# Two transformer layers on one core: in layer 0, exponential before the query's high part, row sum before its low part

## The reference, cut to what matters

```python
q = (query @ Wq + bq).reshape(B, Sq, H, D)
k = (key @ Wk + bk).reshape(B, Sk, H, D)
v = (value @ Wv + bv).reshape(B, Sk, H, D)
scores = jnp.einsum('bqhd,bkhd->bhqk', q, k) * scale
mask = (key_mask == 0)[:, None, None, :]
scores = jnp.where(mask, jnp.float32(-1000000000.0), scores)
probs = jax.nn.softmax(scores, axis=-1)
ctx = jnp.einsum('bhqk,bkhd->bqhd', probs, v).reshape(B, Sq, H * D)
return ctx @ Wo + bo
```

## Time and profile before

| | |
|---|---|
| median of 3 runs | 2923.28 us (2917.49 to 2926.4) |
| the profiled execution's own time | 2921.61 us |
| its span, first to last instruction | 2919.8 us |
| TensorE busy | 2646.1 us (91%) |
| VectorE busy | 2023.6 us (69%) |
| ScalarE busy | 1517.6 us (52%) |
| GpSimd busy | 1522.0 us (52%) |
| TensorE clock granted, mean | 0.953 |

### The profile page before, as it was taken

How to read it: one execution, slowest core, us unless ns; L and a number is a source line. 1 busy time by engine, 2 the same in 40 slices (tenths; PEclk the granted TensorE clock), 3 DMA queues, 4 the chain that set the end, 5 groups by cost and what they waited for, 6 DMA issues and landing times. The chain is left out here.

```text
span 2919.8 us, 41005 instructions
## 1 busy us (share of the span) xinstructions
PE 2646.1 (91%) x14566; PEld 2188.7 (75%) x14566; DVE 2023.6 (69%) x4005; ACT 1517.6 (52%) x2897; POOL 1522.0 (52%) x1149
## 2 busy tenths in 40 slices
PE   6699999986778699999999999999999998799698
PEld 5577777763436588888888888888888887677476
DVE  3677777742546377777777777777777777577666
ACT  2234334331213277777777777777777777111175
POOL 2355544320000166666666666666666666465555
PEclk9899999998878899999999999999999999899899
DMA  5212222133348633334333343233433314668475
GB/s 188 56 54 56 56 57 57 41 96 128 139 145 312 228 74 80 106 83 115 81 77 109 80 118 81 75 111 76 122 80 77 109 51 136 210 238 288 157 275 187
DMA packets 212526, 351.15 MB, mean 120 GB/s; under 512 B 75839, under 2 KB 82370, under 8 KB 204631
## 3 DMA queue, kind: packets, MB, share of 16 engines
q1 hardware_dynamic: 193539, 284.89, 32.8%
q0 software_dynamic: 11680, 45.02, 4.2%
q10 hardware_dynamic: 7104, 18.61, 1.6%
HBM read 172.47 MB, written 156.64 MB: 113 GB/s over the span
## 5 line engine op out<-in xcount | busy, mean ns | idle before, releaser
L1880 POOL TENSOR_SCALAR pa_Pr<-pa_Pr,pa_rs 128x590 f32<-128x590 f32 x512 | 902.4, 1769 | 485.1 <-DVE pa_rs L2109 484.9
L2113 DVE TENSOR_REDUCE pa_least<-pa_S 128x1 f32<-128x590 f32 x512 | 390.7, 763 | 230.0 <-PE pa_S L1944 227.9
L2034 ACT ACTIVATE pa_Pr<-pa_S,pa_least 128x590 f32<-128x590 f32 x512 | 385.5, 753 | 99.4 <-DVE pa_least L2113 96.0
L2066 DVE TENSOR_TENSOR pa_PTl<-pa_W,pa_PTh 128x512 fp32r<-128x512 f32 (+1 forms) x640 | 421.2, 684 | 20.5 <-ACT pa_PTh L2005 16.4
L2005 ACT ACTIVATE pa_PTh<-pa_W 128x512 fp32r<-128x512 f32 (+1 forms) x640 | 367.0, 596 | 58.4 <-PE pa_W L1955 47.1
L1955 PE MATMUL pa_W<-pa_ident,pa_Pr 128*128 128x128 f32 (+1 forms) x2560 | 369.7, 275 | 0.6
L1955 PEld LDWEIGHTS pa_W<-pa_ident,pa_Pr 128*128 128x128 f32 (+1 forms) x2560 | 302.4, 142 | 30.0 <-POOL pa_Pr L1880 2.8
L1971 PE MATMUL pa_O<-pa_PTh,pa_V 128*128 128x512 f32 (+1 forms) x640 | 289.2, 452 | 18.6 <-DVE pa_PTl L2066 14.4
L1972 PE MATMUL pa_O<-pa_PTl,pa_V 128*128 128x512 f32 (+1 forms) x640 | 253.4, 396 | 0.0
L1942 PE MATMUL pa_S<-pa_U,pa_Qh 128*128 128x296 f32 (+1 forms) x1024 | 228.9, 305 | 7.5 <-ACT pa_Pr L2034 0.5
L1942 PEld LDWEIGHTS pa_S<-pa_U,pa_Qh 128*128 128x128 f32 x1024 | 183.2, 188 | 55.5 <-ACT pa_Pr L2034 21.3
(11 more groups left out here) (503 smaller groups left out, 6545.6 us busy)
## 6 DMA issues: line engine op xcount, KB each, us to landing
xs_s<-pa_Ql SPq DMA_DIRECT2D x57, 576.0 KB
pa_Um<-pa_U SPq DMA_DIRECT2D x128, 147.5 KB
pa_Qh<-pa_Qh SPq DMA_DIRECT2D x128, 128.0 KB
o_s<-pa_O_hi SPq DMA_DIRECT2D x64, 256.0 KB, 2.0
o_s<-pa_O_lo SPq DMA_DIRECT2D x64, 256.0 KB, 2.3
Wkv_hi<-o_s SPq DMA_DIRECT2D x8, 2048.0 KB, 11.3
Wkv_lo<-o_s SPq DMA_DIRECT2D x8, 2048.0 KB, 17.0
l_xa<-x SPq DMA_DIRECT2D x8, 1024.0 KB, 6.5
```

What stands on the lines that cost most here:

```text
L1880: pool.tensor_scalar(p, p, rs[:, g % 2, t:t + 1], None, ALU.mult).then_inc(*pool_s.mark("probs", n))
L2034: act.activation(Pr[g % 2][:, t, :], scored[n % 2], ACT.Exp, scale=-1.0, bias=least[:, g % 2, t:t + 1], accum_out=rs[:, g % 2, t:t + 1]).t ...
L2066: dve.tensor_tensor(out, src, f32(hi_ap), ALU.subtract).then_inc(*dve_s.mark(*name))
L2113: dve.tensor_reduce(least[:, g % 2, t:t + 1], scored[n % 2], AX, ALU.min).then_inc(*dve_s.mark("least", n))
```

## The change

Two instructions change their place in each step. On ScalarE the exponential of group s + 1 is written before the high half of the query of group s + 2. On VectorE the row sums and reciprocals of group s + 1 are written before the low half of the query of group s + 2. Nothing else differs; all waits stay as they are with their instructions.

```diff
--- before.py
+++ after.py
@@ -747,13 +747,13 @@
                         act.wait_ge(si_out, 16 * (b - 2))
                     act.activation(si, bank_of["si", b - 2][0:NS, :], ACT.Identity, scale=den[:, 1:2])\
                        .then_inc(*act_s.mark("free", "si", b - 2))
-                if group(s + 2):
-                    d = (s + 2) % C
-                    hi_of(qT[0][:, (s + 2) % QS, :], bank_of["Q", s + 2][:, :], "Q", s + 2, func=ACT.Identity, bias=bq[:, d:d + 1])
                 if group(s + 1):
                     e = (s + 1) % 2
                     act.wait_ge(*dve_s.after("free", "S", s + 1, NT - 1))
                     act.activation(both[:, e, :], both[:, e, :], ACT.Exp, scale=SCALE).then_inc(*act_s.mark("exp", s + 1))
+                if group(s + 2):
+                    d = (s + 2) % C
+                    hi_of(qT[0][:, (s + 2) % QS, :], bank_of["Q", s + 2][:, :], "Q", s + 2, func=ACT.Identity, bias=bq[:, d:d + 1])
                 if group(s):
                     for n in range(2, NK):
                         probabilities_hi(s, n)
@@ -901,9 +901,6 @@
                     shift(s + 1, 3)
                 if c == 2 and batch(b) and batch(b + 2):
                     mask_row(b + 2)
-                if group(s + 2):
-                    d = (s + 2) % C
-                    lo_of(qT[1][:, (s + 2) % QS, :], bank_of["Q", s + 2][:, :], qT[0][:, (s + 2) % QS, :], "Q", s + 2, bias=bq[:, d:d + 1])
                 if new:
                     e = (s + 1) % 2
                     view = both[:, e, :].rearrange("p (q s) -> p q s", s=SK)
@@ -914,6 +911,9 @@
                     dve.reduce_sum(sums, view, AX).then_inc(*dve_s.mark("sum", s + 1))
                     dve.wait_ge(*dve_s.after("sum", s + 1))
                     dve.reciprocal(sums, sums).then_inc(*dve_s.mark("rsum", s + 1))
+                if group(s + 2):
+                    d = (s + 2) % C
+                    lo_of(qT[1][:, (s + 2) % QS, :], bank_of["Q", s + 2][:, :], qT[0][:, (s + 2) % QS, :], "Q", s + 2, bias=bq[:, d:d + 1])
                 if group(s):
                     for n in range(2, NK):
                         probabilities_lo(s, n)
```

## The result

| | before | changed |
|---|---|---|
| median | 2919.45 us (8 runs, 2916.87 to 2926.4) | 2929.84 us (8 runs, 2928.33 to 2935.77) |
| profiled execution, its span | 2919.8 us | 2933.7 us |

The ratio is 1.0027, with a 95% interval of 1.0014 to 1.0040: about 8 us slower, between 4 and 12. The forecast was 2927.0, 5.4 us slower.

What follows compares the result with a forecast made beforehand. TensorE, busy 60.3 of 64 us, was taken to bound layer 0's loop. Third tile -0.4, bank 6 +5.8, clock +1.7 and -1.7 gave +5.4 on 2921.6: 2927.0 us, range 2918 to 2936.

Steps and rivals of the forecast that it cites:

- The bank: Layer 0's loop, steps 10, 14, 18, 22, 26: si waits for bank 6, 2 x 2.09 + 3 x 0.55 = 5.8 us lost.
- The third tile: Waits before read_out(s, 2), steps 0 to 3: 1.48 us gained, then 0.29, 0.51 and 0.29 lost; together 0.4 gained.
- GpSimd: In the loop, GpSimd gets its reciprocals sooner and TensorE hardly waits for it: nothing.
- Steps with c = 0 and 1: Bank 6 causes no new wait there; the tightest, step 9, misses one by 0.18 us.
- The table load: ScalarE, c = 0: falls into idle time, costing nothing; behind its wait, up to 1.1 us in 6 steps, 7 at most.
- The clock: Each 2.09 us wait, steps 10 and 22, has one chance in two of a 1.7 us slow stretch; step 0's stretch goes.
- two terms of the clock: 1.7 us lost behind the two 2.09 us waits, 1.7 us gained as step 0's slow stretch goes.
- case 3: Rival: TensorE's waits for the shift after si shrink by what si cost; 2919.5 us; 15%.
- case 1: Rival: the chain pays in steps 0 to 3, short waits spare the clock; 10.2 us gained, 2912 us; 5%.
- case 2: Rival: the clock falls behind all five si waits; 13.9 us lost, 2935 us; 17%, including a table load behind its wait.
- margins of 0.12 and 0.18: Tile gains only if the last shift ends over 0.12 us before the query's high half; step 9's bank 6 slack 0.18.

Runs made afterwards that it cites:

- si in bank 4: Changed kernel with si of batches 0 to 5 summed in bank 4 instead of 6: 0.9988 of before, 2918.8 us; the old order with the same: 0.9989.
- only the si steps moved: Kernel before with the new order only in steps 10, 14, 18, 22 and 26: 1.0034 of before.
- ScalarE's part alone: Kernel before with only the exponential moved ahead of the query's high half on ScalarE: 1.0025 of before.
- the third tile ahead: Changed kernel with the third tile's low half ahead of the query's low half on VectorE, all groups: 2943.7 us in one execution.
- second profiles: Both kernels timed and profiled once more, unaltered: changed kernel 1.0020 of before, kernel before 0.9987 against itself.
- all but the si steps: Changed kernel with the old order kept in steps 10, 14, 18, 22 and 26: 0.9988 of before.
- VectorE's part alone: Kernel before with only the query's low half moved behind the sums on VectorE: 1.0109 of before, 31 us slower.

## Why the prediction came out as it did

**The bank, right.** The step that carried the sum was that the query's low half, put behind the sums, frees bank 6 too late for si in five steps. Forecast 2 x 2.09 + 3 x 0.55 = 5.8 us; the trace shows 1.94 + 1.93 + 0.39 + 0.51 + 0.39 = 5.2. Both the removal (the si steps alone left in the old order, si in bank 4) and the part by itself (only the si steps moved) show that it makes the loss. The long waits came out 0.15 shorter, and 0.09 of that is the low half itself: I took 0.75 us from the earlier trace rows, and it took 0.66, as the row of step 10 shows. That three of the five waits were short rests on the clock: each of steps 14, 18 and 26 had a stretch at the lower level ahead of it in both profiles. Where one was missing, in the kernels with ScalarE's part alone and with the third tile ahead, such a step waited as long as steps 10 and 22.

**The third tile, right.** Forecast: 1.48 gained in step 0, 0.29 lost in 1 and 3, 0.51 in 2. The waits changed by -1.65, +0.24, +0.42 and, in step 3, from 2.36 to 2.60. In the second profiles they changed by -1.40, +0.27, +0.46 and -0.21; the last has a stretch at the lower clock ahead of it (from 138.3) that the first profile of the change has not. The same 0.66 in place of 0.75 goes toward the differences of 0.1 to 0.2. That the low half stands in the path is shown by the kernel with the tile ahead of it.

**GpSimd, wrong by 0.5 us.** The prediction had nothing there. TensorE came sooner to the tiles of step 1, and waited 0.54 for the multiplied exponentials, which GpSimd makes behind the normalisation of x (109.47 to 111.55, then 111.51 to 113.77). It did so in both profiles of the change, and not with the same order of steps 0 and 1 in the kernels that ran all but the si steps or si in bank 4. So it lies at the edge, and the gain of step 0 was partly capped.

**Steps with c = 0 and 1, right.** No product there waited for bank 6. How near they are is seen from the waits of 0.17 to 0.19 us in five steps with c = 1 when the low half ends 0.6 later, and from the 1.02 in six steps with VectorE's part alone. The table load did go into idle time ahead of its wait, as the earlier trace rows let expect: in step 8 it ran from 213.86 to 215.14, and the exponential waited for the last shift until 216.77. The kernel with VectorE's part alone shows that the load costs nothing only as long as ScalarE's half of the change is made as well.

**The clock, half right.** I gave each wait of 2.09 one chance in two for a stretch at the lower clock, and one in two brought it: step 22 and not step 10, in both profiles of the change. The stretch behind step 0's wait went, as forecast. What I did not see is the rest. Windows of the changed kernel around the ends of its waits of 2.79 (ends at 134.56), 2.60 (146.13), 1.94 (257.02) and 1.93 (464.49), and, ahead of the last, one in which TensorE did not wait at all; columns as above:

```profile
130.00:138.00 8.00, 5.21 (x32) 4.12 (x31) 5.02 (x10) 3.06 (x5) 4.58 (x3) 1.00 0.18 33
146.00:152.00 6.00, 5.87 (x28) 5.42 (x29) 5.06 (x14) 1.65 (x3) 4.02 (x4) 0.72 0.10 16
253.00:262.00 9.00, 7.06 (x35) 3.85 (x34) 3.73 (x9) 3.56 (x7) 7.38 (x4) 1.00 0.42 115
430.00:438.00 8.00, 8.00 (x50) 7.46 (x49) 6.69 (x23) 0.97 (x2) 0.00 (x0) 0.79 0.05 8
463.00:470.00 7.00, 5.51 (x10) 1.63 (x11) 2.20 (x6) 0.73 (x3) 4.84 (x3) 0.76 0.50 146
```

The granted clock stays at 1.00 behind the 2.79 of step 2, where it had fallen behind 2.37 in the kernel before, and falls behind 2.60 and behind the second 1.93. In the second profile of the change it is the other way round in steps 2 and 3: lower from 138.3, behind a wait of 2.83, and not behind one of 2.16. With VectorE's part alone it fell behind two of the five waits of 1.97 to 1.99, and with the third tile ahead behind three of the four of 2.54 to 2.56. So the length of the wait alone doesn't decide, which the step of the prediction took for granted when it placed 2.09 between 1.76 and 2.33. Three low stretches of before are gone from the loop (they began at 112.9, 136.8 and 297.2) and two are new (433.9 and 464.7). Some follow no wait: the stretches from 297.2 and 502.0 before and from 433.9 with the change come with TensorE busy throughout, behind the products of 64 columns of `logits` and the read out, more than 20 us after the last wait. Other steps with the same products have none, so what brings these is open, and so is how much of the clock's part belongs to the waits. In all, the clock's record shows 31 us at the lower level in the loop with the change and 34 before, and 37 and 39 in the second profiles. Within one kernel it differs by 5 to 6 us from run to run, which is 3 us of time. The loop's lengths follow from the waits and half of that time: 5.0 - 1.6 = 3.4, measured 4.1, for the first pair of profiles, and 4.8 - 1.1 = 3.7, measured 4.4, for the second. The rule of the Trainium skill that I set beside it (TensorE: Matmul & The Clock Gate, HAM oscillation), which warns of longer gaps, does not account for these rows: by it none of the new waits would touch the clock, and in step 22 it fell behind a wait of 1.93.

**The size.** +5.4 forecast, +5.8 and +7.9 measured, with intervals of about 4 us to either side. The waits say +4.8 to +5.0, and that this is near the forecast is in part luck: bank 6 came out 0.6 lower than its term, the third tile 0.4 lower, and GpSimd 0.5 higher. The forecast's two terms of the clock cancel, and in the loop the time at the lower level was 2 to 3 us less with the change, so what the ratios hold beyond the waits is not explained by the mechanism. Of the rivals, the absorbed wait (case 3) and the chain that pays everywhere (case 1) are ruled out by the waits. The clock behind every new wait (case 2) did not come, either: one of the five of si.

**What stays open.** The part behind the loop was 2242 us in both profiles of the change and 2237 and 2240 before. In the kernel with the whole change and si in bank 4 it was 2236.9. The runs don't tell whether a part of the measured 6 to 8 us comes from there, and the waits account for 5.

## What to carry to other kernels

When an instruction is moved later in an engine's order, ask what its end releases as well as what it computes: here the low half was off every path as data and on one as the last reader of a bank. Find the next user of that bank in each kind of step, since the loss lay in 5 steps of 32. And if both orders are limited by one bank with two users, give one of them another bank first; then the order hardly matters.

## What was not expected of the hardware

The same subtraction on VectorE, 128x512 with a bias, took 0.75 us in its old place (before, with idle time ahead of it, but also in step 10, directly behind the mask row) and 0.66 behind the reciprocal (the rows of the changed kernel in steps 0 and 10); the prediction's margins of 0.12 and 0.18 are of that size.

TensorE's waits repeat far better than the time: 29.2 us in both profiles of the kernel before, with spans of 2919.8 and 2930.0. The 10 us between those two lie in all three stretches, 2.6 us in the loop, 4.3 in the stretch behind it at a granted clock of 0.83 in place of 0.89, 2.7 in the rest, and the clock's record has 25 us more at the lower level in the second, which is 12 us of time. For a difference of 0.2% in this kernel a sum of waits over a fixed stretch says more than the times of a dozen executions.
